# Pairs of tokens innermost in the FFN's one-hot tiles, and longer loop bodies in the attention and FFN stages

## The chip, the cores and the metric

One NeuronCore of a Trainium2 chip runs the whole program. The metric is the device time of one launch in microseconds. The engines named below are PE (TensorE; PEld is its weight load), DVE (VectorE), ACT (ScalarE), POOL (GpSimd) and SP (SyncE, which issues the DMAs). Each engine runs its own list of instructions in order, and they meet through semaphores.

## The reference, cut to what matters

A batch of 64 images passes a four-layer vision tower, one attention block that keeps the 13 strongest weights of each row, and a product-key feed-forward block (FFN). Only the last two are touched. The FFN, for each of 64 x 198 tokens:

```
q = (x @ Wq + bq).reshape(-1, 8, 128);  q1, q2 = halves of q
s1 = q1 . keys[:, 0];  s2 = q2 . keys[:, 1]            # 8 heads x 64 keys, twice
s1t, i1 = top_k(s1, 8);  s2t, i2 = top_k(s2, 8)
scores, best = top_k(s1t[..., :, None] + s2t[..., None, :], 8)
indices = (i1 * 64 + i2)[best]                          # 64 experts of 4096 per token
inner = x . w_down[indices];  vals = relu(inner) * softmax(scores)
out = sum over the 64 experts of vals * w_up[indices]
```

## The kernel before, in words

The FFN takes 256 tokens a step (`STEP`), as two tiles c = 0, 1 of 128; 12,672 tokens make 50 steps (`NS`). It gathers nothing. PE multiplies the tokens with all of `w_down` (`inner`, L1387, 16 pieces k of 512 columns), ACT applies relu into `f_act` (L1457), DVE multiplies that by a dense matrix of softmax weights, and PE multiplies the result with all of `w_up` (`project`, L1410, 64 matmuls per tile).

The dense matrix of weights, 128 x 32 per token, is made by PE (`weights`, L1399): for every token a product of a one-hot matrix `f_hot` (64 chosen pairs x 128 rows) and a weighted one-hot matrix `f_hotp` (64 x 32 columns), the fp32 weight being split into three bf16 parts that are added up in PSUM. So each unit of 16 tokens (`UNIT`) costs 16 x 3 x 2 = 96 pairs of one weight load (128 columns of bf16) and one matmul (32 columns). Tile c = 0 uses array rows 0 to 63, c = 1 rows 64 to 127. A step has 8 units, u = 0 to 7.

DVE makes the one-hots for a group of 32 tokens (`TG`) in `hot_group`: `f_hotc` (L1614, compares the column number with a table `f_iota`), `f_hotp` (L1622, multiplies it by the three parts of the weight, `f_part`) and `f_hot` (L1625). A step has 4 groups. In these tiles the 32 tokens of the group are innermost. For one token, PE therefore reads elements that lie 32 bf16 numbers, 64 bytes, apart, in the weight load and in the matmul. `split_cols` (L1601 to L1609) writes `f_part` and `f_idx` once a step. The output of a unit is multiplied into `f_act` by `weigh` (L1635), which waits for PE's unit; the rest of DVE's work is the two rounds of top-8 for the next step (L1524 to L1594).

The order of the work is written out by hand. PE, for step n: `project(n-1, c=0)`, unit 0, `project(n-1, c=1)`, unit 1, unit 2, then units 3 to 7, with the transposes, key scores (L1369) and the pieces of `inner` of the following steps between them. DVE, for step n: statistics, `hot_group(1)`, `best_keys`, `weigh(0)`, 16 key numbers, `weigh(1)`, `hot_group(2)`, and so on to `weigh(7)`, `split_cols` and `hot_group(0)` of step n+1. `weigh(u)` can't start before PE's unit u is done; `project(0)` can't start before `weigh(7)` is done.

The FFN's generator `steps` (L1263 to L1272) unrolls the first two and last two steps, and runs the 46 between as a hardware loop of two steps a turn: 23 turns. The attention stage (L879) runs its 64 images as a loop of two images a turn: 32 turns. Every engine has its own copy of the loop and its own branch. In attention DVE, for image n, does `pick(n+1)` (three rounds of MAX8 and MATCH_REPLACE8 over 13 tiles, L1062 and L1067) and then adds the result of image n (L1121).

Of the kernel before, what the change touches and what calls it, by code (L numbers as in the profile page):

```python
# [7 lines left out]
ALU = mybir.AluOpType  # L8
# [797 lines left out]
def build_attention(nc, B, attw_in, h, ident, tokens):  # L806
# [6 lines left out]
    with ExitStack() as ctx:  # L813
# [84 lines left out]
        def _(pe):  # L898
# [67 lines left out]
                front(n)  # L966
                values(n)
            with steps(pe) as it:
                for par in range(2):
                    n = it * 2 + par  # L970
                    front(n + 2)
                    back(n, par)
                    values(n + 2)

        @block.scalar
        def _(act):
# [49 lines left out]
                magnitudes(n, n)  # L1026
                values(n, n)
            with steps(act) as it:
                for par in range(2):
                    n = it * 2 + par  # L1030
                    normalise(n + 2, (n + 2) % B)
                    front(n + 2, par)
                    upto(act, kept, n, 1)
                    act.sem_inc(spare, 1)
                    magnitudes(n + 2, par)
                    back(n)
                    values(n + 2, par)

        @block.vector
        def _(dve):  # L1040
            V = nc.vector
# [71 lines left out]
                statistics(n)  # L1113
            pick(0, 0, 2, first=True)
            with steps(dve) as it:
                for par in range(2):
                    n = it * 2 + par
                    pick(n + 1, 1 - par, (n + 3) % B)
                    upto(dve, proj_ready, n, 1)
                    hp = h[:, bass.ds(n, 1), :, :].rearrange("p i c d -> p (i c d)")  # L1120
                    V.tensor_tensor(hp, hp, PR[:, 0:2 * DIM], ALU.add).then_inc(added.sem, 1)  # L1121
                    upto(dve, added, n, 1)
                    dve.sem_inc(spare, 1)

        @block.gpsimd
        def _(pool):
# [26 lines left out]
            deviations(2)  # L1153
            weigh(0, 0)
            with steps(pool) as it:
                for par in range(2):
                    n = it * 2 + par
# [16 lines left out]
def build_ffn(nc, B, ffnq_in, ffnk_in, ffnb_in, iota_in, wdown_in, wup_in, tokens, out, ident):  # L1174
# [10 lines left out]
    with ExitStack() as ctx:  # L1185
# [77 lines left out]
        def steps(eng):  # L1263

            for n in range(2):
                yield n, 0, n, n + 1 < NS, n + 2 < NS, n > 0
            if NS > 4:
                with eng.Fori(1, NS // 2 - 1) as it:
                    for par in range(2):
                        yield it * 2 + par, it, par, True, True, True  # L1270
            for n in range(max(NS - 2, 2), NS):
                yield n, n // 2, n % 2, n + 1 < NS, n + 2 < NS, True  # L1272

        with ExitStack() as c2:
# [29 lines left out]
            @block.vector  # L1304
            def _(dve):
                for n in range(4):
                    dve.wait_ge(comp_ready, n + 1)
                    src = (IN + AA[0])[n]
                    dst = (wc, bc)[n // 2]
                    nc.vector.tensor_copy(dst[:, (n % 2) * 512:(n % 2) * 512 + 512], src[:]).then_inc(comp_taken, 1)  # L1310
                dve.wait_ge(big_loaded, 48)
                nc.vector.tensor_copy(iota[:], numbers[:].rearrange("p (i o) -> p i o", o=1).to_broadcast([128, 128, TG])
                                      ).then_inc(filled, 1)
# [39 lines left out]
        def _(pe):  # L1353
# [37 lines left out]
            def weights(n, u):  # L1391
                g, slot = u // 2, u % 2
                upto(pe, hot_done, n, g + 1)
                upto(pe, aa_taken[slot], n, u // 2)
                for t in range(UNIT):
                    tt = slot * UNIT + t
                    for pt in range(3):
                        for c in range(2):
                            mm = nc.tensor.matmul(AA[slot][c][:, t * NP:t * NP + NP], hot[64 * c:64 * c + 64, g % 2, :, tt],  # L1399
                                                  hotp[64 * c:64 * c + 64, g % 2, pt, :, tt],  # L1400
                                                  start=(pt == 0), stop=(pt == 2))
                mm.then_inc(aa_ready[slot].sem, 1)

# [80 lines left out]
        def _(dve):  # L1484
# [112 lines left out]
            def split_cols(fr, par):  # L1597

                upto(dve, idx_ready, fr, 1)
                wt = WK[:, 2 * TP:3 * TP]  # L1600
                mark(V.tensor_copy(part[:, par, 0, :], wt))  # L1601
                V.tensor_copy(idx[:, par], WK[:, 0:2 * TP].rearrange("p (n t) -> p n t", n=2))
                met(fr)
                V.tensor_tensor(rest[:, 0], wt, part[:, par, 0, :], ALU.subtract).then_inc(idx_taken.sem, 1)
                upto(dve, idx_taken, fr, 1)
                dve.sem_inc(spare, 1)
                then(V.tensor_copy(part[:, par, 1, :], rest[:, 0]), fr)
                then(V.tensor_tensor(rest[:, 1], rest[:, 0], part[:, par, 1, :], ALU.subtract), fr)
                then(V.tensor_copy(part[:, par, 2, :], rest[:, 1]), fr)  # L1609

            def hot_group(n, par, g):
                t0 = g * TG
                upto(dve, hotp_done, n, g)
                V.tensor_tensor(hotc[:, 0], idx[:, par, 1:2, t0:t0 + TG].to_broadcast([128, NP, TG]), iota[:, 0:NP, :],  # L1614
                                ALU.is_equal).then_inc(hotc_done.sem, 1)
# [206 lines left out]
```

## Time and profile before

| | |
|---|---|
| median of 3 runs | 10608.58 us (10585.94 to 10624.52) |
| profiled execution | 10547.1 us, its span 10545.3 us |
| mean granted TensorE clock | 0.792 |
| tower and norm | 0 to about 5150 us of the span |
| attention | about 5150 to 7000 us |
| FFN | about 7020 to 10545 us |

The page gives each engine's busy time, the span in 40 equal slices (264 us each), and the costliest groups of instructions with the idle time in front of them. PE's granted clock stands in tenths of full speed.

### The profile page before, as it was taken

Reading aid. Unit: us, or ns where it says so; the run is one execution under the profiler, and the core shown is the slowest. Engines: PE = TensorE matmul, PEld = TensorE weight load, DVE = VectorE, ACT = ScalarE, POOL = GpSimd, SP = SyncE. Lnnn points to the kernel's source line nnn. Section 1 sums busy time; section 2 is a strip of 40 time slices with the busy share of each in tenths; the row PEclk is TensorE's granted clock in tenths of the full one; section 3 lists DMA queues with packets and bytes.
Section 4 is the critical chain, followed back from the end, with each engine's and each line's share of the span. In section 5 each row is a group of like instructions: output and inputs, shape, how many; then the busy total and the mean of one; then the engine's idle time right before and its main releaser. Section 6 shows DMA issues by size and latency. Waiting matters only on the chain. (4 is left out here: it accounts for less than half of the span.)

```text
span 10545.3 us, 229521 instructions
## 1 busy us (share of the span) xinstructions
PE 8543.6 (81%) x81842; PEld 6522.5 (62%) x81842; DVE 7228.1 (69%) x25836; ACT 3185.1 (30%) x6691; POOL 1881.5 (18%) x2393
## 2 busy tenths in 40 slices
PE   7777767776777767776377777769999999999999
PEld 7555545554555545554255555558888888888888
DVE  2555545555555545555899999968888888888887
ACT  0333333333333333333244444421111111111111
POOL 0111111111111111111344444410000000000000
PEclk8777777776777767777688888878888888888888
DMA  6322332233223223332000000000000000000000
GB/s 162 38 36 31 38 41 35 31 38 41 33 34 38 35 36 37 38 38 29 3 5 4 5 5 4 4 27 8 8 8 7 8 8 7 8 8 8 7 8 7
DMA packets 349824, 254.32 MB, mean 24 GB/s; under 512 B 38023, under 2 KB 347562, under 8 KB 348493
## 3 DMA queue, kind: packets, MB, share of 16 engines
q1 hardware_dynamic: 348876, 242.70, 15.9%
q8 instruction: 471, 7.72, 0.3%
q14 instruction: 477, 3.90, 0.1%
HBM read 61.50 MB, written 13.04 MB: 7 GB/s over the span
## 5 line engine op out<-in xcount | busy, mean ns | idle before, releaser
L617 DVE TENSOR_REDUCE negmax<-PAIR 99x4 f32<-99x788 f32 x1088 | 1063.9, 978 | 1176.1 <-PE PAIR L373 1037.1
L1399 PEld LDWEIGHTS f_AA<-f_hotp,f_hot 64*128 64x128 bf16 x38400 | 1388.2, 158 | 121.8 <-issue 102.6
L1399 PE MATMUL f_AA<-f_hotp,f_hot 64*128 64x32 bf16 x38400 | 1440.2, 254 | 11.4 <-DVE f_hot L1625 6.9
L373 PE MATMUL PAIR<-ks,qs 96*99 96x198 bf16 x4352 | 809.8, 327 | 675.0 <-DVE negmax L617 570.8
L373 PEld LDWEIGHTS PAIR<-ks,qs 96*99 96x99 bf16 x4352 | 536.8, 166 | 1102.1 <-DVE negmax L617 868.5
L528 ACT ACTIVATE probs<-PAIR 99x792 f32<-99x792 f32 x1024 | 850.3, 830 | 999.8 <-PE PAIR L383 999.1
L1457 ACT ACTIVATE f_act<-f_IN 128x512 f32<-128x512 f32 x800 | 482.2, 603 | 1679.0 <-PE f_IN L1387 1678.8
L1387 PE MATMUL f_IN<-f_zT,f_wd 128*128 128x256 f32 x3200 | 984.0, 469 | 0.0
L1387 PEld LDWEIGHTS f_IN<-f_zT,f_wd 128*128 128x128 f32 x3200 | 760.4, 244 | 291.3 <-issue 138.9
L383 PE MATMUL PAIR<-qs,ks 99*99 99x198 bf16 x4096 | 745.0, 322 | 129.9 <-ACT probs L528 112.9
L1635 DVE TENSOR_TENSOR f_act<-f_act,f_AA 128x512 f32<-128x512 f32 x800 | 510.8, 680 | 483.9 <-PE f_AA L1399 483.8
L1410 PE MATMUL f_OT<-f_wu,f_act 128*128 128x128 f32 x6400 | 786.6, 287 | 56.5 <-issue 56.5
L1410 PEld LDWEIGHTS f_OT<-f_wu,f_act 128*128 128x128 f32 x6400 | 773.5, 203 | 70.2 <-issue 64.8
L383 PEld LDWEIGHTS PAIR<-qs,ks 99*99 99x99 bf16 x4096 | 543.5, 169 | 267.9 <-ACT probs L528 263.7
L399 PE MATMUL WK<-probs,vaug 99*32 99x198 f32 (+1 forms) x8192 | 652.5, 455 | 0.0
L916 PE MATMUL a_SC<-a_kT,a_qm 128*128 128x198 f32 (+1 forms) x1716 | 491.4, 446 | 180.6 <-ACT a_kT L994 162.4
L1721 POOL TENSOR_SCALAR f_nmean<-f_mv 128x2 f32<-128x2 f32 x50 | 20.5, 411 | 3147.8 <-DVE f_mv L1511 3146.6
L916 PEld LDWEIGHTS a_SC<-a_kT,a_qm 128*128 128x128 f32 (+1 forms) x1716 | 396.6, 255 | 281.9 <-ACT a_qm L991 191.5
L1067 DVE MATCH_REPLACE8 a_left<-a_top,a_left 128x198 f32<-128x198 f32 (+1 forms) x1690 | 565.4, 341 | 0.0
L1062 DVE MAX8 a_top<-a_left 128x8 f32<-128x198 f32 (+1 forms) x1690 | 459.9, 342 | 0.0
L1625 DVE TENSOR_TENSOR f_hot<-f_idx,f_iota 128x4096 bf16<-128x4096 bf16 x200 | 456.9, 2284 | 0.0
L1144 POOL TENSOR_TENSOR a_wgt<-a_mag,a_left 128x2574 f32<-128x2574 f32 x65 | 365.9, 5629 | 176.8 <-DVE a_left L1067 176.8
(174 smaller groups left out, 13624.0 us busy)
## 6 DMA issues: line engine op xcount, KB each, us to landing
qs<-parts SPq DMA_DIRECT2D x816, 99.0 KB, 4.3
ks<-parts SPq DMA_DIRECT2D x816, 99.0 KB, 5.4
xbuf<-x_in SPq DMA_DIRECT2D x64, 588.0 KB, 4.4
f_hx<-tokens SPq DMA_DIRECT2D x50, 128.0 KB, 2.5
f_hr<-tokens SPq DMA_DIRECT2D x50, 128.0 KB, 2.3
out<-f_hr SPq DMA_DIRECT2D x50, 128.0 KB, 1.8
qs<-mrows SPq DMA_DIRECT2D x272, 9.3 KB
tokens<-h SPq DMA_DIRECT2D x64, 49.5 KB
```

Source lines behind the costliest of these rows:

```text
L373: mm = nc.tensor.matmul(ps[:, hh, qc * W:qc * W + W], qs[0:STACK, par, 2 * p + hh, j, qc * C:qc * C + C], ks[0:STACK, par, 2 * p + hh, j, ...
L383: mm = nc.tensor.matmul(ps[:, hh, kc * W:kc * W + W], ks[:, par, 2 * p + hh, j, kc * C:kc * C + C], qs[:, par, 2 * p + hh, j, :], start=Tr ...
L399: mm = nc.tensor.matmul(ps[32 * g:32 * g + 32, half * W:half * W + W], vaug[0:keys, par, j, kc, hd, :], probs[0:keys, hd // 2, hd % 2, kc, ...
L528: A.activation(probs[:, p].rearrange("p h k w -> p h (k w)"), ps[:, :, 0:2 * W], ACT.Exp, scale=float(HD) ** -0.5).then_inc(pair_taken[SEA ...
L617: V.tensor_reduce(negmax[:, j, :, 2 * p:2 * p + 2].rearrange("p q h -> p h q"), ps[:, :, 0:2 * W].rearrange("p h (q k) -> p h q k", q=2)[: ...
L916: mm = nc.tensor.matmul(SC[u % 2][0:rows[t], t % 2 * W:t % 2 * W + W], q_rows[:, 128 * t:128 * t + rows[t]], kT[:], start=True, stop=True)
L1067: mr = V.match_replace(left[0:rows[t], par, t, :], top[0:rows[t], t, 8 * r:8 * r + 8], src[0:rows[t], t, :], 0.0)
L1387: mm = nc.tensor.matmul(IN[k % 2][:, m * STEP:m * STEP + STEP], wd[:, 2 * k + m, :], zT[:, par, :], start=True, stop=True)
L1399: mm = nc.tensor.matmul(AA[slot][c][:, t * NP:t * NP + NP], hot[64 * c:64 * c + 64, g % 2, :, tt], hotp[64 * c:64 * c + 64, g % 2, pt, :, tt],
L1410: mm = nc.tensor.matmul(OT[:, c * DIM:c * DIM + DIM], act_in[:, par, k, c * TP:c * TP + TP], wu[:, k, :], start=(k == 0), stop=(k == NP - 1))
L1457: nc.scalar.activation(act_in[:, par, 2 * k:2 * k + 2, :].rearrange("p n w -> p (n w)"), IN[k % 2][:], ACT.Relu).then_inc(inner_taken.sem, 1)
L1635: last = V.tensor_tensor(sl, sl, AA[slot][c][:].rearrange("p (t n) -> p n t", n=NP), ALU.mult)
```

## The change

Two things. First, the layout: tokens are stored in pairs (`TL = 2`), and the pair is innermost, with the row or column number outside it and the 16 pairs of a group outside that. One token's neighbours then lie 2 bf16 numbers, 4 bytes, apart. `f_hot`, `f_hotp`, `f_hotc`, `f_iota` (now 128 x 2) and `f_part` change shape; the number of instructions and the elements of each stay as they were. Second, the loops: `UNROLL = 8` images a turn in attention (8 turns), `TURN = 4` steps a turn in the FFN (11 turns, 2 steps unrolled ahead and 4 behind).

```diff
-        steps = lambda eng: eng.Fori(0, B // 2)
+        UNROLL = 8
+        steps = lambda eng: eng.Fori(0, B // UNROLL)
...
-                for par in range(2):
-                    n = it * 2 + par
+                for k in range(UNROLL):
+                    n, par = it * UNROLL + k, k % 2
...
+TL = 2
+TURN = 4
...
-        iota = sb("f_iota", [128, 128, TG], BF16)
+        iota = sb("f_iota", [128, 128, TL], BF16)
-        part = sb("f_part", [128, 2, 3, TP], BF16)
+        part = sb("f_part", [128, 2, TP // TL, 3, TL], BF16)
-        hotc = sb("f_hotc", [128, 1, NP, TG], BF16)
+        hotc = sb("f_hotc", [128, 1, TG // TL, NP, TL], BF16)
-            if NS > 4:
-                with eng.Fori(1, NS // 2 - 1) as it:
-                    for par in range(2):
-                        yield it * 2 + par, it, par, True, True, True
-            for n in range(max(NS - 2, 2), NS):
+            turns = max((NS - 4) // TURN, 0)
+            if turns:
+                with eng.Fori(0, turns) as it:
+                    for k in range(TURN):
+                        yield it * TURN + (k + 2), it * (TURN // 2) + (1 + k // 2), k % 2, True, True, True
+            for n in range(2 + turns * TURN, NS):
-        hot = sb("f_hot", [128, 2, 128, TG], BF16)
+        hot = sb("f_hot", [128, 2, TG // TL, 128, TL], BF16)
-        hotp = sb("f_hotp", [128, 2, 3, NP, TG], BF16)
+        hotp = sb("f_hotp", [128, 2, TG // TL, 3, NP, TL], BF16)
...
-   matmul(AA[slot][c][...], hot[64 * c:64 * c + 64, g % 2, :, tt],
-                            hotp[64 * c:64 * c + 64, g % 2, pt, :, tt], ...)
+   matmul(AA[slot][c][...], hot[64 * c:64 * c + 64, g % 2, tt // TL, :, tt % TL],
+                            hotp[64 * c:64 * c + 64, g % 2, tt // TL, pt, :, tt % TL], ...)
...
+            def spread(x, k):
+                return x.rearrange("p (a o l) -> p a o l", o=1, l=TL).to_broadcast([128, TG // TL, k, TL])
...
-                V.tensor_tensor(hot[:, g % 2], idx[:, par, 0:1, t0:t0 + TG].to_broadcast([128, 128, TG]), iota[:],
+                V.tensor_tensor(hot[:, g % 2], spread(idx[:, par, 0, t0:t0 + TG], 128),
+                                iota[:].rearrange("p (o n) l -> p o n l", o=1).to_broadcast([128, TG // TL, 128, TL]),
                                 ALU.is_equal).then_inc(hot_done.sem, 1)
```

`f_hotc` and `f_hotp` are built in the same way, and `split_cols` writes its three parts with a row length of 2.

## Rows read from the trace of the kernel before

**Rows 1.** The page: PE's total and the 40 slices of PE, DVE and clock
```profile
PE 8543.6 (81%) x81842; PEld 6522.5 (62%) x81842; DVE 7228.1 (69%) x25836; ACT 3185.1 (30%) x6691; POOL 1881.5 (18%) x2393
PE   7777767776777767776377777769999999999999
DVE  2555545555555545555899999968888888888887
```
**Rows 2.** Windows, attention and FFN: length, busy us (instructions) by engine, clock, DMA
```profile
5000.00:7080.00 2080.00, 1399.31 (x7587) 988.46 (x7588) 1823.73 (x9082) 889.15 (x3127) 816.60 (x444) 0.80 0.02 7
7083.00:10480.00 3397.00, 3328.01 (x46696) 2901.56 (x46695) 2822.78 (x10502) 531.42 (x958) 232.02 (x188) 0.86 0.03 8
```
**Rows 3.** Waits, 5080 to 7080, DVE: who waited for what, us, times, longest
```profile
DVE a_top L1062 <- issue: 125.6, 62, 3.6
```
**Rows 4.** Timeline of DVE in attention: a loop's turn, then no turn
```profile
5229.77 0.40 DVE L1121 TENSOR_TENSOR h<-h,a_PR 99x256 f32 x1
5233.44 1.43 DVE L1062 MAX8 a_top<-a_mag 128x8 f32<-128x198 f32 x5 [3.26 <-issue]
5235.59 0.63 DVE L1062 MAX8 a_top<-a_mag 128x8 f32<-128x198 f32 x2 [0.72 <-issue]
...
5258.76 0.41 DVE L1121 TENSOR_TENSOR h<-h,a_PR 99x256 f32 x1
5259.51 2.76 DVE L1062 MAX8 a_top<-a_mag 128x8 f32<-128x198 f32 x10 [0.34 <-DVE h L1121]
```
**Rows 5.** Waits, 7083 to 10520, PE
```profile
PE f_OT L1410 <- issue: 55.1, 22, 3.2
```
**Rows 6.** Groups by line: xcount, busy us, mean ns of one, idle before
```profile
L1399 PEld LDWEIGHTS f_AA<-f_hotp,f_hot 64*128 64x128 bf16 x38400 | 1388.2, 158 | 121.8 <-issue 102.6
L1399 PE MATMUL f_AA<-f_hotp,f_hot 64*128 64x32 bf16 x38400 | 1440.2, 254 | 11.4 <-DVE f_hot L1625 6.9
```
**Rows 7.** Windows with L1399 alone, one unit each: us, PE, PEld, clock, DMA
```profile
8047.00:8051.00 4.00, 3.57 (x96) 3.41 (x96) 1.00 0.01 4
8822.50:8826.50 4.00, 3.63 (x96) 3.48 (x96) 0.50 0.35 100
9525.50:9529.50 4.00, 3.46 (x96) 3.45 (x96) 0.50 0.33 98
```
**Rows 8.** Timeline of PE in the tower, bf16 matmuls on packed operands
```profile
2001.51 0.54 PE L373 MATMUL PAIR<-ks,qs 96*99 96x198 bf16 x4 [0.38 <-DVE negmax L617]
2012.14 0.90 PE L373 MATMUL PAIR<-ks,qs 96*99 96x198 bf16 x4 [5.22 <-DVE negmax L617]
```
**Rows 9.** L1635 (`weigh`), 7083 to 10480: what ended its idle time
```profile
  PE f_AA L1399: 462.7, 197
```
**Rows 10.** Timeline in the FFN, two steps up to the second unit
```profile
8030.71 1.28 DVE L1635 TENSOR_TENSOR f_act<-f_act,f_AA 128x512 f32<-128x512 f32 x2 [7.89 <-PE f_AA L1399]
...
8074.99 7.31 PE L1410 MATMUL f_OT<-f_wu,f_act 128*128 128x128 f32 x64
8082.23 3.60 PE L1399 MATMUL f_AA<-f_hotp,f_hot 64*128 64x32 bf16 x96
8085.76 7.41 PE L1410 MATMUL f_OT<-f_wu,f_act 128*128 128x128 f32 x64
8096.79 1.28 DVE L1635 TENSOR_TENSOR f_act<-f_act,f_AA 128x512 f32<-128x512 f32 x2 [2.89 <-PE f_AA L1399]
...
8145.65 10.31 PE L1410 MATMUL f_OT<-f_wu,f_act 128*128 128x128 f32 x64 [2.70 <-issue]
```
**Rows 11.** Groups by line: the DVE operations of `hot_group`, and two fp32 ones
```profile
L1625 DVE TENSOR_TENSOR f_hot<-f_idx,f_iota 128x4096 bf16<-128x4096 bf16 x200 | 456.9, 2284 | 0.0
L1622 DVE TENSOR_TENSOR f_hotp<-f_hotc,f_part 128x3072 bf16<-128x3072 bf16 x200 | 351.7, 1758 | 6.9
L1614 DVE TENSOR_TENSOR f_hotc<-f_idx,f_iota 128x1024 bf16<-128x1024 bf16 x200 | 136.3, 681 | 10.7 <-DVE f_part L1609 10.1
L1532 DVE TENSOR_TENSOR f_pairs<-f_top 128x1024 f32<-128x1024 f32 x50 | 60.3, 1207 | 0.0
L1575 DVE TENSOR_REDUCE f_got<-f_sc 128x256 f32<-128x2048 f32 x50 | 113.8, 2276 | 0.1
```

More of the change, by code:

```diff
@@ L1028, in _ @@
             with steps(act) as it:
-                for par in range(2):
-                    n = it * 2 + par
+                for k in range(UNROLL):
+                    n, par = it * UNROLL + k, k % 2
                     normalise(n + 2, (n + 2) % B)
@@ L1115, in _ @@
             with steps(dve) as it:
-                for par in range(2):
-                    n = it * 2 + par
+                for k in range(UNROLL):
+                    n, par = it * UNROLL + k, k % 2
                     pick(n + 1, 1 - par, (n + 3) % B)
@@ L1155, in _ @@
             with steps(pool) as it:
-                for par in range(2):
-                    n = it * 2 + par
+                for k in range(UNROLL):
+                    n, par = it * UNROLL + k, k % 2
                     deviations(n + 3)
@@ L1266, in steps @@
                 yield n, 0, n, n + 1 < NS, n + 2 < NS, n > 0
-            if NS > 4:
-                with eng.Fori(1, NS // 2 - 1) as it:
-                    for par in range(2):
-                        yield it * 2 + par, it, par, True, True, True
-            for n in range(max(NS - 2, 2), NS):
+            turns = max((NS - 4) // TURN, 0)
[4 more added lines that the diff above has]
+            for n in range(2 + turns * TURN, NS):
                 yield n, n // 2, n % 2, n + 1 < NS, n + 2 < NS, True
@@ L1311, in _ @@
                 dve.wait_ge(big_loaded, 48)
-                nc.vector.tensor_copy(iota[:], numbers[:].rearrange("p (i o) -> p i o", o=1).to_broadcast([128, 128, TG])
+                nc.vector.tensor_copy(iota[:], numbers[:].rearrange("p (i o) -> p i o", o=1).to_broadcast([128, 128, TL])
                                       ).then_inc(filled, 1)
                 dve.wait_ge(comp_taken, 4)
-        hot = sb("f_hot", [128, 2, 128, TG], BF16)
+        hot = sb("f_hot", [128, 2, TG // TL, 128, TL], BF16)
         act_in = sb("f_act", [128, 2, NP, STEP])
-        hotp = sb("f_hotp", [128, 2, 3, NP, TG], BF16)
+        hotp = sb("f_hotp", [128, 2, TG // TL, 3, NP, TL], BF16)
         block = ctx.enter_context(nc.Block())
@@ L1398, in weights @@
                         for c in range(2):
-                            mm = nc.tensor.matmul(AA[slot][c][:, t * NP:t * NP + NP], hot[64 * c:64 * c + 64, g % 2, :, tt],
-                                                  hotp[64 * c:64 * c + 64, g % 2, pt, :, tt],
+                            mm = nc.tensor.matmul(AA[slot][c][:, t * NP:t * NP + NP], hot[64 * c:64 * c + 64, g % 2, tt // TL, :, tt % TL],
+                                                  hotp[64 * c:64 * c + 64, g % 2, tt // TL, pt, :, tt % TL],
                                                   start=(pt == 0), stop=(pt == 2))
@@ L1599, in split_cols @@
                 upto(dve, idx_ready, fr, 1)
-                wt = WK[:, 2 * TP:3 * TP]
-                mark(V.tensor_copy(part[:, par, 0, :], wt))
+                wt = WK[:, 2 * TP:3 * TP].rearrange("p (a l) -> p a l", l=TL)
+                piece = lambda k: part[:, par, :, k, :]
+                left = lambda k: rest[:, k].rearrange("p (a l) -> p a l", l=TL)
+                mark(V.tensor_copy(piece(0), wt))
                 V.tensor_copy(idx[:, par], WK[:, 0:2 * TP].rearrange("p (n t) -> p n t", n=2))
                 met(fr)
-                V.tensor_tensor(rest[:, 0], wt, part[:, par, 0, :], ALU.subtract).then_inc(idx_taken.sem, 1)
+                V.tensor_tensor(left(0), wt, piece(0), ALU.subtract).then_inc(idx_taken.sem, 1)
                 upto(dve, idx_taken, fr, 1)
                 dve.sem_inc(spare, 1)
-                then(V.tensor_copy(part[:, par, 1, :], rest[:, 0]), fr)
-                then(V.tensor_tensor(rest[:, 1], rest[:, 0], part[:, par, 1, :], ALU.subtract), fr)
-                then(V.tensor_copy(part[:, par, 2, :], rest[:, 1]), fr)
+                then(V.tensor_copy(piece(1), left(0)), fr)
+                then(V.tensor_tensor(left(1), left(0), piece(1), ALU.subtract), fr)
+                then(V.tensor_copy(piece(2), left(1)), fr)
+            def spread(x, k):
+                return x.rearrange("p (a o l) -> p a o l", o=1, l=TL).to_broadcast([128, TG // TL, k, TL])
             def hot_group(n, par, g):
@@ L1613, in hot_group @@
                 upto(dve, hotp_done, n, g)
-                V.tensor_tensor(hotc[:, 0], idx[:, par, 1:2, t0:t0 + TG].to_broadcast([128, NP, TG]), iota[:, 0:NP, :],
+                V.tensor_tensor(hotc[:, 0], spread(idx[:, par, 1, t0:t0 + TG], NP),
+                                iota[:, 0:NP, :].rearrange("p (o n) l -> p o n l", o=1).to_broadcast([128, TG // TL, NP, TL]),
                                 ALU.is_equal).then_inc(hotc_done.sem, 1)
@@ L1621, in hot_group @@
                 upto(dve, hotc_done, n, g + 1)
-                V.tensor_tensor(hotp[:, g % 2], hotc[:].to_broadcast([128, 3, NP, TG]),
-                                part[:, par, :, t0:t0 + TG].rearrange("p (k o) t -> p k o t", o=1).to_broadcast([128, 3, NP, TG]),
+                e = 3 * t0 // TL
+                V.tensor_tensor(hotp[:, g % 2], hotc[:].rearrange("p o a n l -> p a o n l").to_broadcast([128, TG // TL, 3, NP, TL]),
+                                part[:, par].rearrange("p a k l -> p (a k) l")[:, e:e + 3 * TG // TL].rearrange(
+                                    "p (e o) l -> p e o l", o=1).to_broadcast([128, 3 * TG // TL, NP, TL]).rearrange(
+                                        "p (a k) n l -> p a k n l", k=3),
                                 ALU.mult).then_inc(hotp_done.sem, 1)
-                V.tensor_tensor(hot[:, g % 2], idx[:, par, 0:1, t0:t0 + TG].to_broadcast([128, 128, TG]), iota[:],
+                V.tensor_tensor(hot[:, g % 2], spread(idx[:, par, 0, t0:t0 + TG], 128),
+                                iota[:].rearrange("p (o n) l -> p o n l", o=1).to_broadcast([128, TG // TL, 128, TL]),
                                 ALU.is_equal).then_inc(hot_done.sem, 1)
```

## The prediction

> **What bounds the kernel now.** I read the slices first [rows 1]. They split the span in three: a tower in which PE is some 70% busy and DVE about half, then six slices in which DVE stands at 8 or 9, then thirteen in which PE stands at 9 and DVE at 8. The change touches the last two. The windows put numbers on them [rows 2]. In the 2080 us around attention DVE is busy for 1824; nothing else passes 1400. In 48 steps of the FFN (3397 us, 70.8 us a step) PE is busy for 3328 (69.3 a step) and DVE for 2823 (58.8 a step). So attention runs at DVE's pace, and the FFN at PE's, with DVE 17% behind it. That second number is a ceiling on whatever PE gains.
>
> Then the waits. In attention the largest wait of DVE that lies within the images is "issue", 125.6 us in 62 pieces, in front of the first MAX8s of an image [rows 3]. The timeline shows where: at the turn of the loop DVE ends L1121 at 5229.77 + 0.40 and stands for 3.26 us and again for 0.72; after the next image, with no turn, the same place costs 0.34 [rows 4]. 62 pieces are two for each of the 31 backward branches. In the FFN PE has the same kind of gap ahead of `project`, 55.1 us in 22 pieces, one for each of the 22 backward branches [rows 5, 10], seen at 8145.65.
>
> DVE's waits in the FFN are almost all of `weigh` for PE's units: 462.7 us, 9.6 a step [rows 9]; the remaining 70.8 - 58.8 - 9.6 = 2.4 us a step are small latencies.
>
> **The loops.** Attention goes from 31 backward branches to 7. Each costs 125.6 / 31 = 4.05 us of DVE, less the 0.34 that an unturned image pays there: 3.7 us. DVE is dense otherwise, so the full amount is on the path: 24 x 3.7 = 89 us. The FFN goes from 22 to 10. Each costs PE 55.1 / 22 = 2.5 us ahead of the first `project`, on the way to the second unit, for which DVE waits: 12 x 2.5 = 30 us. The bounds: none of it comes back, if the gap came from something that straight code has as well (against it: the turn-free image of [rows 4], 0.34); or a little more, the whole 4.05 and 2.8. The code that the longer bodies and two more unrolled steps add costs nothing that I can see: the instructions run are the same in number. SP's loops are Python loops already and do not change. Sum of the loops: 119 us.
>
> **The layout, on PE.** One unit is 96 weight loads and 96 matmuls. It takes 3.41 to 3.48 us of weight load, 36 ns a pair, and what matters is when: 3.41 at the full clock of 2.4 GHz (1.00) and 3.45 to 3.48 at 1.2 GHz (0.50) [rows 7]. A stream bound by the array changes with the clock, as the packed bf16 matmuls of the tower do: four in 0.54 us at one level and 0.90 at the other [rows 8]. So what holds the units is not the array. What is particular to them is that both operands are read at steps of 64 bytes, and that is what the change removes. From above: it removes nothing, 36 ns stay. From below: the packed stream's (0.54 - 0.25) / 3 = 97 ns for 198 columns (0.25 us being the length of one, [rows 6]) makes 16 ns for 32 columns. PE also has to load 128 weight columns each time, for which `project` (64 pairs in 7.31 us, 114 ns, with 128 fp32 columns each way, [rows 10]) gives 29 ns for a quarter of the columns. I take 25 ns: between the ends, near that last row. A unit then takes 2.4 us in place of 3.46: 1.06 us less, 8.5 us a step.
>
> The Trainium skill, "SBUF — State Buffer", section "Door 1: The DMA port swizzle", says that SBUF is read in lines of 16 bytes and that an access pays when fewer than two hits fall on a line. By it a step of 64 bytes (one hit a line) pays and a step of 4 (four hits) does not, which is the forecast's side; the clock-blind pace of rows 7 agrees, though no row has these operands packed.
>
> **What of 8.5 us a step arrives.** Two parts. (1) From the end of `weigh(7)` to the second unit PE runs `project`, unit 0, `project`, unit 1 [rows 10]; DVE arrives there 2.9 us early in an undisturbed step and 7.9 where `project` ran after a turn and partly at 1.2 GHz. I put the mean at 5.5 us. Two units lie on that way, so 2.1 us go and about 3.4 stay. (2) The other 9.6 - 5.5 = 4.1 us are waits at the later units, where PE is just behind; six units shorter by 1.06 make 6.4, more than there is, so all 4.1 go and DVE sets the pace. Together 6.2 us; I take 6.0, since the turns' gaps of (1) are already in the 30. 48 x 6.0 = 288 us. The step becomes 64.8 us, less the turns; PE would be busy 60.8 of them, so it fits.
>
> **The layout, on DVE.** Same elements, same number of operations. `f_hot`, `f_hotp` and `f_hotc` now run over rows of two elements. Their rate is (2284 - 681) / 3072 = 0.52 ns an element; the fp32 operations run at (2276 - 1207) / 1024 = 1.04 [rows 11]. So the bf16 ones take two elements a tick now. I cost the rows of two at nothing: the pair is still adjacent in all three operands, and in L1575 rows of eight cost nothing at a row's end. The bounds are zero and the one-element rate (the slow rival below). The writes of `split_cols` in rows of two: zero to 0.1 us on each of four operations, under 20 us in all, and hidden while PE is in `project`.
>
> The Trainium skill, "Vector Engine (DVE) Microarchitecture Reference", section 5.1, asks for a unit step and more than one element in the innermost dimension for the two-element rate of 2-byte operands; rows of two meet that, so by it DVE stays as it is. No row shows rows of two.
>
> **Sum.** 89 + 30 + 288 = 407 us. The profiled execution took 10547 us and would take 10140. The median of the runs is 61 us above it, so I forecast 10608 - 407 = 10201, say 10200 us.
>
> **Rivals.**
> (B) The layout does not do what it says: 36 ns is the price of loading weights for so short a matmul, whatever the step. For it: no row shows a packed bf16 pair under 36 ns. Against it: the price would not follow the clock at all. Only the loops pay: 10608 - 119 = 10489 us.
> The Trainium skill, "TensorE: Matmul & The Clock Gate", section "Weight-path perf modes", gives about 40 ns a matmul for small ones with the fast weight load; if that is a floor here too, the outcome is B, and the measured 36 ns agrees as well with it as with the step.
> (C) The units reach the lower bound, 16 ns, 1.54 us a unit, 1.92 less. On way (1) 3.8 us go, on way (2) 4.1: 7.9 x 48 = 379, with the loops 498: 10110 us. If `project` also runs at 2.4 GHz more often because PE is denser, DVE's floor is 58.8 + 2.4 = 61.2 us a step, 9.6 x 48 + 89 = 550: 10060 us.
> (D) Slower: DVE's read of a two-element row with a repeated outer step falls to one element a tick. Price: 0.52 ns x 8192 elements = 4.3 us a group, 17.1 a step. DVE becomes the bound with 58.8 + 17.1 + 2.4 = 78.3 us a step, 7.5 x 48 = 360 more, less 89 of attention: 10608 + 271 = 10880 us. It decides once a group costs (9.6 + 89 / 48) / 4 = 2.9 us more, about two thirds of that. For it: no row shows two sources in rows of two. Against it: the repeated operand of L1622 runs at the fast rate already.
> (E) PE, with more gaps, is granted 1.2 GHz in more of the FFN. `project` in rows 10 takes 10.3 in place of 7.3 where it ran partly there; 3 us more a step is 144 us: 10345 us.
>
> **How the numbers follow.** Forecast 0.46, B 0.24, C 0.13, D 0.10, E 0.07. A measurement of this kernel tells 0.3%, 32 us, from no change. The forecast, C and E are faster by more, and B by 119 us as well; only if B and a failure of the loop gain come together is it the same, which I give 0.03 of B's 0.24. Faster 0.87, same 0.03, slower 0.10. The range goes from 10060 (C's end) to 10500 (B's); beyond it lie D and a few hundredths of B and C.
>
> **What would show it.** In the FFN: units of 96 pairs in about 2.4 us at either clock (3.46 is B, 1.5 is C); L1625 and its two sisters still at 2284, 1758 and 681 ns (4.4 us is D); `weigh` waiting some 3 us a step in place of 9.6; DVE's share of the FFN above 90%. In attention: issue waits of DVE in 14 pieces, some 28 us. The prediction is wrong if the units stay at 3.46, if the DVE operations lengthen, or if straight bodies show issue gaps of their own.

## The result: 10037 us, 5.3% faster, just below the forecast's range

The changed kernel takes 10036.92 us (median of 4, 10021.63 to 10053.81), beside 10597.26 for the kernel before on the same chip: a ratio of 0.9473 [0.944, 0.9506]. The forecast was 10200 us with a range from 10060. The sign was right; the gain is 560 us where 407 was forecast. One execution of the kernel before, in a later comparison, took 21236 us at a granted clock of 0.305 and is left out there.

The page of the changed kernel, with the lines that answer to [rows 1] and the clock:

```profile
PE 7459.7 (74%) x81842; PEld 5526.4 (55%) x81842; DVE 7189.9 (72%) x25836; ACT 3176.1 (32%) x6691; POOL 1881.0 (19%) x2393
PE   7777767777677776777637777776777777777777
DVE  2555545555455554555589999997999999999998
PEclk8676777777677776777768888887888888888888
```

PE lost 1084 us of busy time and DVE only 38. In the last twelve slices PE fell from 9 to 7 and DVE rose from 8 to 9: the two changed places. The windows of the changed kernel, attention and 47 steps of the FFN, answer to [rows 2]:

```profile
5000.00:6990.00 1990.00, 1383.67 (x7910) 993.08 (x7912) 1828.60 (x9125) 887.99 (x3132) 814.36 (x444) 0.81 0.03 8
6970.00:9900.00 2930.00, 2270.61 (x45726) 1908.66 (x45725) 2732.28 (x10287) 517.05 (x940) 231.49 (x188) 0.87 0.03 9
```

DVE is now busy for 2732 of 2930 us in the FFN, 93%. Per step (2930 / 47 = 62.3 us) that is 58.1 of DVE and 48.3 of PE, where before it was 58.8 and 69.3 of 70.8. The groups by line of the changed kernel answer to [rows 6, 11] (L1403 was L1399, L1649 was L1635, and the last three were L1625, L1622 and L1614):

```profile
L1403 PE MATMUL f_AA<-f_hotp,f_hot 64*128 64x32 bf16 x38400 | 546.6, 174 | 194.6 <-DVE f_act L1649 159.0 <-issue 28.4 <-DVE f_hot L1638 6.9
L1403 PEld LDWEIGHTS f_AA<-f_hotp,f_hot 64*128 64x128 bf16 x38400 | 510.5, 94 | 295.4 <-issue 271.6 <-DVE f_hot L1638 11.2
L1649 DVE TENSOR_TENSOR f_act<-f_act,f_AA 128x512 f32<-128x512 f32 x800 | 510.1, 680 | 132.8 <-PE f_AA L1403 132.8
L1638 DVE TENSOR_TENSOR f_hot<-f_idx,f_iota 128x4096 bf16<-128x4096 bf16 x200 | 456.9, 2285 | 0.0
L1633 DVE TENSOR_TENSOR f_hotp<-f_hotc,f_part 128x3072 bf16<-128x3072 bf16 x200 | 351.6, 1758 | 6.9
L1623 DVE TENSOR_TENSOR f_hotc<-f_idx,f_iota 128x1024 bf16<-128x1024 bf16 x200 | 136.7, 684 | 10.5 <-DVE f_part L1615 9.6
```

The weight loads of the units went from 1388.2 to 510.5 us of busy time. Divided by 38400, a pair went from 36.2 to 13.3 ns, and that quotient is called the pace below. DVE's three operations did not move. PE now waits for DVE ahead of the units (159.0 us; before, [rows 6] leave at most 11.4 - 6.9 = 4.5 for it). The timeline of PE in one step of the changed kernel, beside [rows 10]:

```profile
7969.92 7.31 PE L1414 MATMUL f_OT<-f_wu,f_act 128*128 128x128 f32 x64
7977.16 1.37 PE L1403 MATMUL f_AA<-f_hotp,f_hot 64*128 64x32 bf16 x96
7978.45 7.41 PE L1414 MATMUL f_OT<-f_wu,f_act 128*128 128x128 f32 x64
...
7999.00 1.37 PE L1403 MATMUL f_AA<-f_hotp,f_hot 64*128 64x32 bf16 x96 [3.50 <-DVE f_act L1649]
8007.53 2.07 PE L1373 MATMUL f_WK<-f_wc,f_zT 128*128 128x512 f32 x2 [7.16 <-DVE f_sc L1521]
```

And single units of the changed kernel, in windows with L1403 alone (us, PE, PEld, clock, DMA), beside [rows 7]:

```profile
7977.00:7978.60 1.60, 1.37 (x96) 1.27 (x96) 1.00 0.00 0
8438.20:8440.20 2.00, 1.60 (x96) 1.46 (x96) 0.50 0.03 8
```

**Where the 560 us come from.** Attention is measured from the first to the last of the 64 additions (L1121, now L1122), the FFN from the first to the last `project` matmul (L1410, now L1414). Both come from the starts that the view of one line gives. For the two kernels here and four of the experiments, one profiled execution each:

| kernel | attention, us | FFN, us |
|---|---|---|
| before | 1709.2 | 3458.4 |
| new loops, old layout | 1619.4 | 3456.8 |
| new layout, old loops | 1708.3 | 3083.0 |
| the change | 1618.9 | 3043.7 |
| the change, executed again later | 1618.2 | 3047.5 |
| no loops at all | 1587.8 | 3005.0 |

The change took 90.3 us from attention and 414.7 from the FFN, 505 together. These two stages repeat well: the changed kernel's two profiled executions differ by 0.7 and 3.8 us in them. The rest of the span was another 20.5 us shorter, 525.5 in all, and 14 of these lie ahead of attention's first addition, where the tower has no edit: attention's first addition began at 5204.5 us before and at 5190.2 in the changed kernel, but at 5250.7 in the changed kernel's second profiled execution. The last 35 us lie in the comparison: the profiled execution of the kernel before was 50 us faster than its median, that of the changed one 15. So 55 of the 560 us stand in neither of the two edited stages, and no run explains them.

### The profile page after: what moved, and what is told of

The parts are those of the page before. It is cut to its first block and busy times, and to the rows that moved or that the text cites. A ratio compares the mean times of both kernels' runs of the same rounds, so it can differ in the third digit from the quotient of the medians.

```text
span 10019.8 us, 228107 instructions
## 1 busy us (share of the span) xinstructions
PE 7459.7 (74%) x81842; PEld 5526.4 (55%) x81842; DVE 7189.9 (72%) x25836; ACT 3176.1 (32%) x6691; POOL 1881.0 (19%) x2393
## 5 line engine op out<-in xcount | busy, mean ns | idle before, releaser
L1391 PE MATMUL f_IN<-f_zT,f_wd 128*128 128x256 f32 x3200 | 900.7, 438 | 1.8 <-issue 1.7
L1391 PEld LDWEIGHTS f_IN<-f_zT,f_wd 128*128 128x128 f32 x3200 | 694.8, 224 | 256.0 <-issue 125.6
L1414 PE MATMUL f_OT<-f_wu,f_act 128*128 128x128 f32 x6400 | 743.8, 278 | 21.9 <-issue 21.9
L1414 PEld LDWEIGHTS f_OT<-f_wu,f_act 128*128 128x128 f32 x6400 | 734.3, 194 | 33.9 <-issue 28.5
L1403 PE MATMUL f_AA<-f_hotp,f_hot 64*128 64x32 bf16 x38400 | 546.6, 174 | 194.6 <-DVE f_act L1649 159.0
L1403 PEld LDWEIGHTS f_AA<-f_hotp,f_hot 64*128 64x128 bf16 x38400 | 510.5, 94 | 295.4 <-issue 271.6
L1649 DVE TENSOR_TENSOR f_act<-f_act,f_AA 128x512 f32<-128x512 f32 x800 | 510.1, 680 | 132.8 <-PE f_AA L1403 132.8
L917 PEld LDWEIGHTS a_SC<-a_kT,a_qm 128*128 128x128 f32 (+1 forms) x1716 | 416.8, 265 | 280.2 <-ACT a_qm L992 194.6
L1373 PE MATMUL f_WK<-f_wc,f_zT 128*128 128x512 f32 x400 | 278.0, 783 | 346.9 <-DVE f_sc L1521 346.0
L1638 DVE TENSOR_TENSOR f_hot<-f_idx,f_iota 128x4096 bf16<-128x4096 bf16 x200 | 456.9, 2285 | 0.0
```

Of the source, the lines that this page charges most:

```text
L917: mm = nc.tensor.matmul(SC[u % 2][0:rows[t], t % 2 * W:t % 2 * W + W], q_rows[:, 128 * t:128 * t + rows[t]], kT[:], start=True, stop=True)
L1391: mm = nc.tensor.matmul(IN[k % 2][:, m * STEP:m * STEP + STEP], wd[:, 2 * k + m, :], zT[:, par, :], start=True, stop=True)
L1414: mm = nc.tensor.matmul(OT[:, c * DIM:c * DIM + DIM], act_in[:, par, k, c * TP:c * TP + TP], wu[:, k, :], start=(k == 0), stop=(k == NP - 1))
L1638: V.tensor_tensor(hot[:, g % 2], spread(idx[:, par, 0, t0:t0 + TG], 128), iota[:].rearrange("p (o n) l -> p o n l", o=1).to_broadcast([128 ...
L1649: last = V.tensor_tensor(sl, sl, AA[slot][c][:].rearrange("p (t n) -> p n t", n=NP), ALU.mult)
```

## The experiments

### The two halves apart

Rival B said that the layout does nothing. Each half was run without the other. (This diff and those below are against the changed kernel.)

```diff
 # new loops, old layout
-TL = 2
+TL = 32
 # new layout, old loops
-        UNROLL = 8
+        UNROLL = 2
-TURN = 4
+TURN = 2
```

> The old layout (32 tokens innermost, TL = 32) with the new loops of 8 images and 4 steps. If the loops' part of the forecast was right, it is 119 us faster than before: attention 24 backward branches x 3.7 us = 89, FFN 12 x 2.5 = 30; units of 96 pairs still take 3.46 us. Rival: the loops gave the surplus that the forecast missed (560 measured against 407), then it is some 250 us faster, and the FFN's step falls below 69 us.

> The new layout with the old loops of 2 images and 2 steps. If the two parts add up, it is about 560 - 119 = 440 us faster than before. If the backward branch costs DVE, the new bound of the FFN, less than it cost PE (DVE's branch is hidden behind its queue), the 12 extra branches of the FFN cost under 30 us here and it is 450 to 460 us faster. Units take 1.3 us.

New loops alone: 10485.74 us, ratio 0.9898 [0.9877, 0.9919]. New layout alone: 10185.59, ratio 0.9621 [0.9605, 0.9637]. By ratio these are 108 us (86 to 130) and 401 us (384 to 418) of the kernel before in that comparison (10581). The loops' 119 lies in its interval; the layout alone brought less than the 440 expected, and the two halves add up to 509 and not to 560. Rival B fell: the layout carries most of it. The groups by line, of the new loops alone first, then of the new layout alone:

```profile
L1403 PEld LDWEIGHTS f_AA<-f_hotp,f_hot 64*128 64x128 bf16 x38400 | 1388.5, 158 | 118.8 <-issue 99.6 <-DVE f_hot L1638 7.3
L1649 DVE TENSOR_TENSOR f_act<-f_act,f_AA 128x512 f32<-128x512 f32 x800 | 511.2, 681 | 479.2 <-PE f_AA L1403 478.7
```

```profile
L1403 PEld LDWEIGHTS f_AA<-f_hotp,f_hot 64*128 64x128 bf16 x38400 | 511.9, 94 | 268.7 <-issue 238.8 <-DVE f_hot L1638 17.7
L1649 DVE TENSOR_TENSOR f_act<-f_act,f_AA 128x512 f32<-128x512 f32 x800 | 510.9, 682 | 160.7 <-PE f_AA L1403 160.7
```

The pace belongs to the layout alone. The table above holds something else: in attention the loops bring 90 us with either layout, in the FFN 1.6 with the old one and 39.3 with the new one. The windows of the new loops alone show where the first went, in 48 steps, to be read against the second line of [rows 2]:

```profile
7028.00:10423.00 3395.00, 3351.18 (x46696) 2922.27 (x46695) 2827.06 (x10504) 531.48 (x958) 231.52 (x188) 0.85 0.03 8
```

PE stands idle for 44 us in place of 69, so the branches' gaps did go (its "issue" wait before `project` fell from 55.1 us to 27.5). But the same 46696 matmuls are busy for 23 us more at a granted clock of 0.85 in place of 0.86: the gain was used up by matmuls at the lower clock. Whether the shorter gaps cause that, or the two executions merely differ by it, one profile of each cannot say. By the medians the FFN's share of the loops there is the rest, 108 - 90 = 18 us, give or take 22, so the 30 of the forecast are not excluded.

### Which of the two reads pays

A unit reads `f_hot` (the weight load) and `f_hotp` (the matmul) at the same step. Here one is in pairs and the other still in 64-byte steps; `f_hotc` and the parts follow `f_hotp`.

```diff
+TH = 2     # 32 in the reverse, where TL = 2
-TL = 2
+TL = 32
...
-        hot = sb("f_hot", [128, 2, TG // TL, 128, TL], BF16)
+        hot = sb("f_hot", [128, 2, TG // TH, 128, TH], BF16)
```

> New loops; f_hot (the weights that PE loads) in pairs, 4 bytes between neighbours; f_hotp and f_hotc (the moving 32 columns) as before, 64 bytes. Theory 1, the weight load alone held the units: the pair falls from 36 to 13 ns, about 10040 us. Theory 2, the moving operand held them: the pair stays at 36 ns, 10490 us. Theory 3, both reads pay one after the other: about 25 ns, 10150 to 10200 us.

> New loops; f_hotp, f_hotc and f_part in pairs, f_hot as before at 64 bytes. Theory 1 (weight load alone): the pair stays at 36 ns, 10490 us. Theory 2 (moving operand alone): 13 ns, 10040 us. Theory 3 (one after the other): about 25 ns, 10150 to 10200 us. If both this and the kernel with packed f_hot stay at 36 ns, the two reads run side by side at the same slow pace.

`f_hot` in pairs: 10316.5 us, 0.975 [0.9731, 0.9769]. `f_hotp` in pairs: 10356.66 us, 0.9788 [0.9772, 0.9805]. The two lines of the unit, with `f_hot` in pairs, then with `f_hotp` in pairs:

```profile
L1406 PE MATMUL f_AA<-f_hotp,f_hot 64*128 64x32 bf16 x38400 | 1168.6, 233 | 16.0 <-DVE f_act L1652 9.0 <-DVE f_hot L1641 6.9
L1406 PEld LDWEIGHTS f_AA<-f_hotp,f_hot 64*128 64x128 bf16 x38400 | 1110.1, 112 | 113.9 <-issue 84.6 <-DVE f_hot L1641 17.5
```

```profile
L1406 PE MATMUL f_AA<-f_hotp,f_hot 64*128 64x32 bf16 x38400 | 1265.0, 211 | 14.8 <-DVE f_act L1652 7.9 <-DVE f_hot L1641 6.9
L1406 PEld LDWEIGHTS f_AA<-f_hotp,f_hot 64*128 64x128 bf16 x38400 | 1231.4, 164 | 115.5 <-issue 92.3 <-DVE f_hot L1641 11.3
```

Read the mean of one instruction first. With `f_hot` in pairs the weight load falls from 158 to 112 ns; with `f_hotp` in pairs the matmul falls from 254 to 211 and the weight load stays at 164. So each read has a price of its own. (Ends of matmuls are modelled in a profile, so the pace, which comes from the weight loads, weighs more.) Then the pace: 28.9 and 32.1 ns, against 36.2 with neither and 13.3 with both. One packed read brings 7.3 or 4.1 of the 22.9 ns, and both bring all. If the two prices were paid one after the other, they would add up: 15.6 ns for the moving read (28.9 - 13.3) and 18.8 for the weight read (32.1 - 13.3) would make 47.7 with neither packed, and it is 36.2. If the slower read alone set the pace, neither packed would be 32.1. So the reads run mostly beside each other, and most of the pace is the slower one's; how they share the last 4 ns is not shown. None of the three theories that I had written down holds; a change that packs only one operand gets less than half of the gain (the FFN took 3284.9 and 3343.5 us, 172 and 113 less than with the old layout, against 413 for both).

### How wide a step

TL is the number of tokens that are innermost, and twice that the bytes between a token's neighbours.

```diff
-TL = 2
+TL = 4     # 8 bytes; TL = 8: 16 bytes; TL = 16: 32 bytes; TL = 1: 2 bytes
```

> The changed kernel with TL = 4: both operands of the units at 8 bytes between neighbours. Line theory (PE pays when a 16-byte line serves fewer than two of its reads): two reads a line, so it stays at 13 ns a pair and about 10040 us. Step theory (the price grows with every byte of the step): between 13 and 36, say 15 to 18 ns, and still about 10040 to 10080 us since DVE is the bound.

> TL = 8: 16 bytes between neighbours, one read a line. Line theory: the full 36 ns of the kernel before, 10490 us. Step theory: some 18 to 22 ns, about 10100 to 10150 us.

> TL = 16: 32 bytes. Line theory: no different from 16 and 64 bytes, 36 ns, 10490 us. Step theory: 25 to 28 ns, about 10200 to 10300 us.

> TL = 1: 2 bytes between neighbours for PE, but rows of one element for DVE. This makes the slow rival of the prediction happen: f_hot 4.4 us, f_hotp 3.35, f_hotc 1.2, that is 4.3 us a group and 17.1 a step more on DVE. If DVE bounds the changed kernel, all of it arrives: 49 x 15.5 to 17 = 760 to 840 us over the changed kernel's 10037, so 10800 to 10870, slower than before. If DVE had slack of some us a step (PE bound), less arrives, 10700 or under. PE's pair stays at 13 ns by both theories.

Each of the four ran twice and was profiled once. Ratios to the kernel before: 8 bytes 0.9565 [0.9505, 0.9624], 16 bytes 0.9763 [0.9703, 0.9822], 32 bytes 0.9774 [0.973, 0.9819], 2 bytes 1.0203 [1.0146, 1.026]. The weight loads of 8, 16 and 32 bytes, one kernel each:

```profile
L1403 PEld LDWEIGHTS f_AA<-f_hotp,f_hot 64*128 64x128 bf16 x38400 | 670.8, 114 | 246.9 <-issue 225.8 <-DVE f_hot L1638 9.3
```

```profile
L1403 PEld LDWEIGHTS f_AA<-f_hotp,f_hot 64*128 64x128 bf16 x38400 | 1221.4, 156 | 115.9 <-issue 92.8 <-DVE f_hot L1638 11.3
```

```profile
L1403 PEld LDWEIGHTS f_AA<-f_hotp,f_hot 64*128 64x128 bf16 x38400 | 1301.2, 153 | 121.9 <-issue 102.7 <-DVE f_hot L1638 7.3
```

| bytes between neighbours | pace, ns | FFN, us | median, us |
|---|---|---|---|
| 2 | 13.5 | 3826.9 | 10836.39 |
| 4 (the change) | 13.3 | 3043.7 | 10036.92 |
| 8 | 17.5 | 3138.0 | 10158.52 |
| 16 | 31.8 | 3344.5 | 10368.96 |
| 32 | 33.9 | 3358.9 | 10381.42 |
| 64 (new loops alone) | 36.2 | 3456.8 | 10485.74 |

The pace jumps by 14.3 ns between 8 and 16 bytes and by 4.4 in all from there to 64. That is not a smooth function of the step but a threshold with two small slopes beside it, and neither of the two theories in the expectations had it so: the line theory put 8 bytes at 13 ns and 16 and 32 bytes at 36, the step theory put 16 bytes at 18 to 22. The Trainium skill, "SBUF — State Buffer", section "Door 1: The DMA port swizzle", puts the threshold at two hits on a line of 16 bytes, which for neighbours means a step of 8 bytes or less. The jump agrees with it; the 4.2 ns between 4 and 8 bytes, where both have two hits or more, and the slope beyond 16 do not follow from it.

At 2 bytes PE keeps its pace and DVE loses its own. The three operations in that kernel:

```profile
L1638 DVE TENSOR_TENSOR f_hot<-f_idx,f_iota 128x4096 bf16<-128x4096 bf16 x200 | 883.6, 4418 | 0.0
L1633 DVE TENSOR_TENSOR f_hotp<-f_hotc,f_part 128x3072 bf16<-128x3072 bf16 x200 | 671.6, 3358 | 6.8
L1623 DVE TENSOR_TENSOR f_hotc<-f_idx,f_iota 128x1024 bf16<-128x1024 bf16 x200 | 242.9, 1214 | 10.5 <-DVE f_part L1615 9.6
```

They take 4.26 us a group more, 853 us over 200 groups, and the FFN is 783 us longer than in the changed kernel (3826.9 against 3043.7), the median 799. This is rival D's mechanism at rival D's price (4.3 us a group, 10880 us forecast, 10836 measured), in rows of one instead of two. Of what DVE gets longer, 92% arrives in the FFN.

DVE isn't the only engine that counts, though. At 8 bytes 10040 to 10080 us were expected, since DVE was taken for the bound, and the median is 10158.52. The pace is 4.2 ns longer there, which makes 157 us of PE in 49 steps of 768 pairs, and the FFN is 94 us longer: 60% of what PE gets longer arrives too.

### What bounds the kernel now

If DVE is the bound, two things should help: no branch at all, and work taken off DVE. The changed kernel was run again beside them (10043.99 us, 0.9475 [0.9439, 0.951]; no edit).

```diff
 # no loops
-        UNROLL = 8
+        UNROLL = 64
-TURN = 4
+TURN = 46
 # f_hotp of groups 2 and 3 on GpSimd
+        PG = (2, 3)
...
+                if g in PG:                             # PE, ahead of the group's first unit
+                    upto(pe, hotp_done, n, g + 1)
...
+                if g not in PG:
+                    weighted(V, par, g).then_inc(hotp_done.sem, 1)
...
+                for g in PG:
+                    upto(pool, aa_ready[1], n, g - 1)
+                    upto(pool, hotc_done, n, g + 1)
...
+                    weighted(nc.gpsimd, par, g).then_inc(hotp_done.sem, 1)
```

> The changed kernel once more, as the measure of the three that follow: 10037 us, 0.947 of before.

> The changed kernel with UNROLL = 64 and TURN = 46: no backward branch is left in attention or the FFN. If a branch costs 3.7 us of DVE in attention and about 1.7 us a step in the FFN (between the 2.5 us of PE's gap before and what DVE's queue hides), 7 x 3.7 + 10 x 1.7 = 43 us go: 9995 us. Rival: the straight code is so long that fetching it costs as much as the branches did: no difference.

> The changed kernel with f_hotp of groups 2 and 3 made by POOL in place of DVE: 2 x 1.76 = 3.5 us a step less on DVE. If DVE bounds the FFN, 49 x 2.5 to 3.5 = 120 to 170 us go: 9870 to 9920 us. If PE's own chain (project, two units, project) is what is left, under 50 us go. Rival: POOL is too slow (over 10 us for 3072 elements) or slows DVE by sharing its port, then nothing is won or it gets slower.

> Both of the last two edits. If they are independent, their gains add: about 9830 to 9880 us.

No loops: 9990.62 us (9979.44 to 10006.04), 0.9421 [0.9385, 0.9457]. It beats both kernels, the changed one by 53 us, where 43 were expected. In the profiled executions attention gained 31.1 us for 7 branches and the FFN 38.7 for 10.

GpSimd with half of `f_hotp`: 10129.68 us, 0.9559 [0.9523, 0.9596], slower than the change by 86 us; with no loops as well 10072.23, 0.9508 [0.9471, 0.9546], slower by 82 than no loops alone. The expectations (9870 to 9920, and 9830 to 9880) missed, and their rival, that GpSimd slows DVE, came true. The groups by line of that kernel (L1547 was L1536, L1562 was L1551):

```profile
L1328 POOL TENSOR_TENSOR f_hotp<-f_hotc,f_part 128x3072 bf16<-128x3072 bf16 x100 | 734.8, 7348 | 910.6 <-DVE f_hotc L1634 901.2 <-issue 9.4
L1562 DVE TENSOR_TENSOR f_ex<-f_best 128x128 f32<-128x128 f32 x50 | 237.5, 4750 | 0.1
L1328 DVE TENSOR_TENSOR f_hotp<-f_hotc,f_part 128x3072 bf16<-128x3072 bf16 x100 | 175.8, 1758 | 3.4
L1547 DVE TENSOR_TENSOR f_pairs<-f_top 128x1024 f32<-128x1024 f32 x50 | 144.4, 2889 | 0.0
```

In the changed kernel the same two short ones were:

```profile
L1536 DVE TENSOR_TENSOR f_pairs<-f_top 128x1024 f32<-128x1024 f32 x50 | 60.3, 1206 | 0.0
L1551 DVE TENSOR_TENSOR f_ex<-f_best 128x128 f32<-128x128 f32 x50 | 14.2, 283 | 0.1
```

DVE was relieved of 351.6 - 175.8 = 175.8 us, and these two took 223 + 84 = 307 us more. So DVE was not relieved in this run, and it says nothing on whether a relieved DVE would end earlier. The timeline of that kernel shows how:

```profile
8028.70 7.35 POOL L1328 TENSOR_TENSOR f_hotp<-f_hotc,f_part 128x3072 bf16<-128x3072 bf16 x1 [9.41 <-DVE f_hotc L1634]
8034.21 2.91 DVE L1547 TENSOR_TENSOR f_pairs<-f_top 128x1024 f32<-128x1024 f32 x1
...
8042.38 2.29 DVE L1645 TENSOR_TENSOR f_hot<-f_idx,f_iota 128x4096 bf16<-128x4096 bf16 x1
8042.53 7.35 POOL L1328 TENSOR_TENSOR f_hotp<-f_hotc,f_part 128x3072 bf16<-128x3072 bf16 x1 [6.48 <-DVE f_hotc L1634]
8045.19 4.83 DVE L1562 TENSOR_TENSOR f_ex<-f_best 128x128 f32<-128x128 f32 x1
```

GpSimd's second operation ends at 8049.88; `f_ex`, 0.28 us of work, begins at 8045.19 and ends at 8050.02. `f_pairs`, 1.2 us of work, ends 1.07 after GpSimd's first. Both have two inputs in SBUF. The profile books the standing as busy time, so DVE looks fuller, not idle. The order counts: `f_hot` (L1645) has two inputs in SBUF as well and runs beside GpSimd's operation in groups 2 and 3, but it begins 0.15 us ahead of it, and it takes 2.29 us as ever. How much of GpSimd's 7.35 us is standing behind `f_hot` no run shows. The Trainium skill, "SBUF — State Buffer", section "Who interferes with whom", says that such a DVE instruction takes its second input through the read interface it shares with GpSimd, and that one blocks the other. The rows of `f_pairs` and `f_ex` agree.

## Why the prediction was right in kind and short in size

**Attention's loops: right.** 24 branches at 3.7 us, 89 us; measured 90.3. In the changed kernel's attention the issue wait is what was to be seen, 14 pieces and 29.3 us:

```profile
DVE a_top L1063 <- issue: 29.3, 14, 3.7
```

**The FFN's loops: near in size, but not a term by itself.** 30 us were forecast, and 39.3 are there with the new layout. With the old one the profiled executions give 1.6. The sum had the term as independent of the layout, and it isn't.

**The sum against the stages.** The gain is 153 us above the forecast. With the loops first and the layout on top, attention gave 1 us more than forecast, the FFN's loops 28 less (1.6), and the layout 125 more (413 in place of 288). The other 55 are those that stand in neither stage.

**The pace of a pair: the step that failed.** I took 25 ns, between 36 and a lower bound of 16. It is 13.3, under the bound.

The 25 leaned on the row of `project`, 114 ns for 128 columns of fp32, of which I took a quarter for 32 columns of bf16. The tower's rows had the bf16 price: two of its matmuls of 198 columns start 84 ns apart at the full clock in the trace (2001.725 and 2001.809), 0.42 ns a column, where `project` pays 0.89. A quarter of `project`'s columns at the bf16 price is 13.6 ns and not 29.

The bound of 16 was worked out wrongly as well. The four matmuls of 0.54 us start 125, 88 and 84 ns apart; I averaged the first distance in, and the 0.25 us that I took off for the length of one is the length of another matmul (the units', [rows 6]). The last distance gives 13.6 ns for 32 columns, close to what came.

At the lower clock, though, even that is no bound. There the tower's matmuls start 163 to 166 ns apart, which makes 27 ns for 32 columns, and the units of the changed kernel start one matmul every 13.5 ns. What differs is that the tower has one stream of matmuls and the units have two: c = 0 on array rows 0 to 63 and c = 1 on rows 64 to 127. In the start times of the changed kernel's units at the full clock the second of the two matmuls mostly starts 3 ns after the first, and the next two 22 ns after that: 25 ns for two. At the lower clock it is 27 ns for two. (In the kernel before it was 71.) I had named the two row groups in the description of the kernel and did not price them. That the second stream makes the difference is read from these starts; no run has the units on one row group.

**What of it arrives: overestimated, which hid part of the error.** I had 6.0 of 8.5 us a step arriving at 25 ns. Between the FFN times at 28.9 ns (3284.9 us) and at 17.5 ns (3138.0) a straight line gives 3235 us at 25 ns (an estimate), 222 us less than the new loops with the old layout, where I had 288. So by this estimate the conversion was 66 us too high, and the step from 25 to 13.3 ns was worth 191 more: 288 - 66 + 191 = 413, the 3456.8 - 3043.7 of the tables.

Which of the two parts failed can be read from DVE's idle time ahead of each unit's two `weigh` operations, summed from their starts and ends in the traces, in us a step:

| kernel, pace | unit 1 | unit 5 | units 6, 7 | all |
|---|---|---|---|---|
| before, 36.2 ns | 5.3 | 2.5 | 1.6 | 9.5 |
| new loops, old layout, 36.2 | 5.0 | 2.9 | 1.5 | 9.4 |
| 16 bytes, 31.8 | 3.2 | 3.1 | 1.1 | 7.4 |
| `f_hot` in pairs, 28.9 | 3.0 | 3.1 | 0.6 | 6.7 |
| 8 bytes, 17.5 | 2.1 | 2.2 | 0.0 | 4.4 |
| the change, 13.3 | 1.3 | 1.2 | 0.0 | 2.6 |

Way (1) was sound: 5.5 us were assumed and 5.3 are there, and it fell at least as far as forecast (3.4). Part (2) failed. The waits of units 6 and 7 went, but that of unit 5, the largest of the later ones, did not fall between 36.2 and 28.9 ns (2.9 to 3.1 with the new loops) and gave way only below that. Units 2 to 4 have no wait in any of these kernels, so a faster unit there does not by itself shorten a wait of DVE. I had counted all six later units against one sum of waits. Why unit 5 holds on so long no run shows.

**DVE unchanged: right for the three operations, not for the stage.** 2285, 1758 and 684 ns, against 2284, 1758 and 681 in [rows 11]. But of the layout's 413 us only 372 are idle time of DVE in the FFN; the other 41 are busy time (2856.0 us with the old layout, 2815.4 with the new). The sum had no such term. Half of it is one operation that no edit touches, the comparison and multiplication of `f_rankf` and `f_topf` (L1572), whose mean fell from 448 to 405 ns, 19.7 us of busy time; why, no run shows.

**The rivals.** C is nearest to what happened, at 0.13: pace at or below its end, `project` at the full clock more often, and DVE busy for most of the step. That its numbers nearly hold is in part luck. The floor was to be 58.8 of busy time and 2.4 of latencies, 61.2 us a step; the step is 62.3, of 58.1 busy, 2.6 still waiting at `weigh` and 1.6 of the rest. The FFN was to give 461 us and gave 415; the time was to be 10060 and is 10037 only because 55 us came from outside the two stages. `project` and `inner` did run faster, as C's second half says. Their groups in the kernel before, then in the changed one:

```profile
L1387 PE MATMUL f_IN<-f_zT,f_wd 128*128 128x256 f32 x3200 | 984.0, 469 | 0.0
L1410 PE MATMUL f_OT<-f_wu,f_act 128*128 128x128 f32 x6400 | 786.6, 287 | 56.5 <-issue 56.5
```

```profile
L1391 PE MATMUL f_IN<-f_zT,f_wd 128*128 128x256 f32 x3200 | 900.7, 438 | 1.8 <-issue 1.7
L1414 PE MATMUL f_OT<-f_wu,f_act 128*128 128x128 f32 x6400 | 743.8, 278 | 21.9 <-issue 21.9
```

None of their lines was edited, and 83 + 43 = 126 us of their busy time went. By start times and the clock's records 484 of the 6400 `project` matmuls started in the lower clock before, and 74 in the changed kernel; of the 3200 of `inner` 1143 and 699. The mean granted clock of the stretch only went from 0.86 to 0.87, since the lower clock now falls more on PE's waits: 5 of 952 us at the lower clock had PE idle before, and 351 of 792 now. E had the sign of that wrong. B is excluded by the layout alone, and D by the unchanged DVE operations, though its price is real one step further, at rows of one.

The Trainium skill, "TensorE: Matmul & The Clock Gate", section "Weight-path perf modes", stood behind B with about 40 ns for a small matmul, which the page gives for fp8. The 36.2 ns of before agreed with it as well as with the step; the 13.3 ns after do not. It is no floor here.

**The range.** Its lower end was C's end. C's two bounds, 16 ns and DVE's floor, were treated as hard. The pace was not, and the floor was not reached. The 23 us by which the result lies under 10060 are less than the result's own interval, which reaches from 0.944 to 0.9506 (10060 is 0.9493), and less than the 55 us outside the stages. So the miss of the range by itself says little; the 25 ns in place of 13.3 is what was wrong.

## What to carry to other kernels

Before giving a rate to short matmuls, look at three things: the byte step at which each operand is read, the type of the row that the rate comes from, and whether neighbours use different array rows. A step of 16 bytes or more cost 32 to 36 ns a pair here, 8 bytes 17.5 and 4 bytes 13, and both operands had to be packed for it. A rate from an fp32 row was twice too high for bf16. When an engine is sped up past its neighbour, sum up the neighbour's busy time in the stage first: that floor (61.2 us forecast, 62.3 measured) forecast the end better than the rate did. Choose the inner length for all readers: rows of two were the shortest that kept DVE's rate and the fastest on PE.

## What the runs showed of the hardware that I had not expected

- The pace by byte step, 13.3 at 4, 17.5 at 8, 31.8 at 16, 33.9 at 32 and 36.2 ns at 64 bytes, is a threshold with slopes, and weight read and matmul read mostly overlap, so that packing one alone brings 7.3 or 4.1 of 22.9 ns.
- Two matmuls on different array rows mostly start 3 ns apart at the full clock; a packed pair on 64 rows costs 13.3 ns with the other half of the array busy too. Its clock dependence is small: 1.27 us a unit at a granted clock of 1.00, 1.46 at 0.50.
- A DVE operation with two inputs in SBUF that begins behind GpSimd's tensor operation stands until that is over (283 ns became 4750), and the profile counts it as busy. One that began 0.15 us ahead of it did not lengthen (`f_hot`, 2.29 us). FIND_INDEX8 at 219 ns and the addition of `f_bc` with an input in PSUM (L1532 there, 684 ns), which ran beside GpSimd's operation, did not lengthen either.
- A backward branch cost DVE 3.8 to 4.4 us in attention (90.3 / 24, 31.1 / 7) and the FFN 3.3 to 3.9 us each with the new layout (39.3 / 12, 38.7 / 10).
